# A float32 cross-attention kernel: q is loaded ahead of the first keys' lifts, and the scores of head 1 stand behind the following context product

## The reference

```python
query = hidden_states @ Wq
keyt = enc @ Wk
valt = enc @ Wv
hs = _mha(query, keyt, valt)            # softmax(q k^T / sqrt(80)) v, per head
ca_q1 = jnp.einsum('btc,th->bch', ca, Wq_ca)[:, indices, :]
ca_hs1 = _mha(ca_q1, residual, residual)
ca_hs2 = _mha(ca_hs1 @ Wq, ca @ Wk_ca, ca @ Wv_ca)
out = (hs + ca_hs2) @ Wout + b_out + residual
```

## Time and profile before

| | us |
|---|---|
| median of 3 runs | 1008.68 |
| lowest and highest | 1005.97, 1013.66 |
| the profiled execution, its own time | 1004.1 |
| its span, from the first to the last instruction | 1002.4 |

### The profile page before, as it was taken

How to read it: one execution, slowest core, us unless ns; L and a number is a source line. 1 busy time by engine, 2 the same in 40 slices (tenths; PEclk the granted TensorE clock), 3 DMA queues, 4 the chain that set the end, 5 groups by cost and what they waited for, 6 DMA issues and landing times.

```text
span 1002.4 us, 20729 instructions
## 1 busy us (share of the span) xinstructions
PE 983.8 (98%) x6740; PEld 964.2 (96%) x6740; DVE 645.5 (64%) x1129; ACT 490.0 (49%) x895; POOL 343.5 (34%) x286
## 2 busy tenths in 40 slices
PE   9999799999999999999999999999999999999998
PEld 9998699999999999999999999999999999998997
DVE  6444556676667766767676767676766666667444
ACT  7433445555454546464646463646454545546110
POOL 5212254424251616151524243343343343416000
PEclk9899999999999999999999999999999999999999
DMA  7989967797978797979797978888787878795354
GB/s 266 258 285 279 259 131 203 168 196 172 195 172 191 174 182 178 185 184 179 185 186 176 186 191 169 202 174 201 161 208 157 206 163 202 168 216 156 97 181 146
DMA packets 154169, 190.12 MB, mean 190 GB/s; under 512 B 80928, under 2 KB 108192, under 8 KB 154144
## 3 DMA queue, kind: packets, MB, share of 16 engines
q1 hardware_dynamic: 147456, 177.44, 75.9%
q10 hardware_dynamic: 6688, 12.35, 3.7%
HBM read 81.56 MB, written 19.95 MB: 101 GB/s over the span
## 4 chain that ended last, share of the span: by engine, by line
PE 85%; SPq 5%; DMA 4%; DVE 3%; ACT 2%; issue 1%; ACTq 0%
PE psS L750 22%; PE psB L785 20%; PE psB L790 10%; PE psS L725 8%; PE psT L766 6%; PE psS L894 6%; PE psT L812 4%; PE psT L818 2%; SPq L382 2%; DMA kstack<-kT 1%; PE psB L867 1%; PE psB L844 1%; SPq L379 1%; PE psT L819 1%; PE psS L950 1%
## 5 line engine op out<-in xcount | busy, mean ns | idle before, releaser
L750 PE MATMUL psS<-encT_keep,Wk_keep 128*128 128x360 f32 x1440 | 255.3, 330 | 2.8 <-ACT probs L1133 2.8
L750 PEld LDWEIGHTS psS<-encT_keep,Wk_keep 128*128 128x128 f32 x1440 | 238.7, 189 | 3.9 <-issue 3.3
L785 PE MATMUL psB<-PT_h,encN_h 120*128 120x400 f32 x576 | 202.3, 351 | 0.0
L785 PE MATMUL psB<-PT_l,encN_h 120*128 120x400 f32 x576 | 198.8, 345 | 0.0
L1133 ACT ACTIVATE probs<-psS,negmax 100x718 f32<-100x718 f32 x128 | 110.2, 861 | 131.8 <-DVE negmax L1524 131.6
L612 POOL TENSOR_TENSOR encT_keep<-encT_raw,encT_keep 128x718 fp32r<-128x718 f32 x45 | 79.7, 1770 | 184.6 <-ACT encT_keep L1162 182.2
L1548 DVE TENSOR_TENSOR kT<-psS,kT 128x718 fp32r<-128x718 f32 x80 | 72.4, 905 | 105.7 <-ACT kT L1157 105.7
L620 POOL TENSOR_TENSOR encN_l<-enc_raw,encN_h 120x768 fp32r<-120x768 f32 x48 | 92.4, 1926 | 93.5 <-ACT encN_h L1169 92.1
L603 POOL TENSOR_TENSOR Mbd<-Mbd,fmask 128x320 fp32r<-128x320 f32 x48 | 47.0, 978 | 221.4 <-DMA Mbd<-m_split 218.8
L1157 ACT ACTIVATE kT<-psS 128x718 fp32r<-128x718 f32 x80 | 61.7, 771 | 123.4 <-PE psS L750 109.9
L790 PE MATMUL psB<-PT_h,encN_l 120*128 120x400 f32 x576 | 120.4, 344 | 0.7 <-POOL encN_l L620 0.7
(11 more groups left out here) (245 smaller groups left out, 1635.8 us busy)
## 6 DMA issues: line engine op xcount, KB each, us to landing
kstack<-kT SPq DMA_DIRECT2D x64, 448.8 KB
kstack<-kT SPq DMA_DIRECT2D x192, 112.2 KB
enc_raw<-in_encN_dram SPq DMA_DIRECT2D x48, 360.0 KB, 5.5
encT_raw<-in_encT_dram SPq DMA_DIRECT2D x45, 359.0 KB, 6.0
kstack<-kT SPq DMA_DIRECT2D x32, 359.0 KB
kstack<-kT SPq DMA_DIRECT2D x32, 269.2 KB
kstack<-kT SPq DMA_DIRECT2D x32, 179.5 KB, 3.6
kstack<-kT SPq DMA_DIRECT2D x64, 89.8 KB, 3.9
```

What stands on the lines that cost most here:

```text
L750: mm = pe.matmul(keys_in(f, first)[:, half, 0:HALF], w[:, c, f * 128:(f + 1) * 128], e[:, c, k0:k0 + HALF], start=(j == 0), stop=(j == 3 * ...
L785: pe.matmul(psB[:, 1, 0:RH], eN[0][:, k, cc], PT[p][:, k, rows], start=(k == 0 and p == 0), stop=False)
```

## The change

SyncE issues `load_q(i + 1)` ahead of `lift(i + 1, 0)` in the batches that are not the first. Head 1 of the next batch leaves the end of `batch(i)` on PE, ACT and DVE and goes into the start of `batch(i + 1)`: `scores(i, 1)` behind `context(i - 1, 2)`, `expo(i, 1)` behind `u_high(i - 1, 2)`, `rowmax(i, 1)` behind `u_low(i - 1, 2)`. On DVE `norm(i, 1)` also goes behind `k_low(i, 3)`. No instruction is added or removed, and no wait.

```diff
--- before.py
+++ after.py
@@ -528,9 +528,9 @@
                         if not last:
                             store_hs(i - 1, 1)
                     if not last:
-                        lift(i + 1, 0)
                         if not first:
                             load_q(i + 1)
+                        lift(i + 1, 0)
                         lift(i + 1, 1)
                         if first:
                             sp.wait_ge(s["q"], NP * GROUPS)
@@ -1005,6 +1005,7 @@
                 def batch(i, first=False, last=False):
                     if not first:
                         context(i - 1, 2)
+                        scores(i, 1)
                     keys(i, 3)
                     if not first:
                         values(i - 1, 0)
@@ -1069,7 +1070,6 @@
                         context(i, 1)
                         scores(i + 1, 0)
                         b2_scores(i + 1, 1)
-                        scores(i + 1, 1)
 
                 pe.wait_ge(s["warm"], 2)
                 warm = gbd[:, 0:4, :].rearrange("p h j -> p (h j)")
@@ -1296,6 +1296,7 @@
                 def batch(i, first=False, last=False):
                     if not first:
                         u_high(i - 1, 2)
+                        expo(i, 1)
                     k_high(i, 3)
                     if first:
                         store_q2(4, FT)
@@ -1396,7 +1397,6 @@
                         u_high(i, 1)
                         expo(i + 1, 0)
                         b2_exp(i + 1)
-                        expo(i + 1, 1)
 
 
                 for c in range(2):
@@ -1685,8 +1685,9 @@
                     b2_norm(i)
                     if not first:
                         u_low(i - 1, 2)
+                        rowmax(i, 1)
+                    k_low(i, 3)
                     norm(i, 1)
-                    k_low(i, 3)
                     if first:
                         q_low(3, 0)
                     else:
@@ -1761,7 +1762,6 @@
                         u_low(i, 1)
                         rowmax(i + 1, 0)
                         b2_less_max(i + 1, 1)
-                        rowmax(i + 1, 1)
 
 
                 nc.vector.memset(st2[:, 0, :], 0.0).then_inc(s["warm"], 1)
```

## The result

The changed kernel takes 1016.74 us in the median of 18 runs (1013.27 to 1022.95), the kernel before 1009.35 in 18 runs taken beside it. The ratio is 1.0075, 95% interval 1.0058 to 1.0092: slower by 0.75%, some 7.6 us. One of the 18 executions of the kernel before took 2957 us; without it their median would be 1008.68. The forecast was 1.8%, 18 us. The sign and the mechanisms were right, the size was not, and the main reason is one term of the sum.

What follows compares the result with a forecast made beforehand. PE, busy 983.8 of 1002.4 us, was taken to bound the kernel. 14 x (1.0 + 0.3) = 18.2, plus 0.3 and 0.4, less 1.0, gave +17.9, rounded to 18: 1008.7 + 18 = 1027 us, range 1012 to 1038.

Steps and rivals of the forecast that it cites:

- at most 1.0 us could be won: In the loop, 14 batches at 52.00 us against the best batch's 51.93 leave at most 1.0 us to gain.
- the waits at `values`: PE's weight load of `values` waits for `u_low(i, 2)` behind `b2_norm`; the change removes this, gaining 1.0 us.
- Part 1: At the batch boundary, q issued ahead of the lift of f = 0: about 1.0 us lost in each of 14 batches.
- 0.8 us in hand: Before L832's second half on PE: `b2_less_max(0)` is done 0.85 us early, so some 1.0 of 1.8 us remains.
- The shares of 0.76 and 1.04: DMA shares at the boundary, lift f = 0 at 0.76, then q at 1.04; read as trace agreement on queue order.
- a landing near 506.5: Estimate from the skill page alone for the lift at the boundary: lands near 506.5, without any wait.
- I take 1.8: Lateness of `k_high(i + 1, 2)` behind the lift at each loop boundary, taken from the end of batch 0: 1.8 us.
- The bounds in the text, 0 to 1.5: Cost per boundary of the later lift: 0 if it lands after 2.4 us, about 1.5 us if after 6.8.
- Part 2: Head 1's scores behind `context(i - 1, 2)` uncover the psB evacuation: 0.6 us a batch alone, 0.3 behind a stalled L832.
- the +0.4 of the last batch: In the last batch, SyncE's lifts and the load of Wout follow `hs_add`, maybe 0.4 us later: +0.4 once.
- A: At the boundaries, the lift lands in time and only lost cover costs, 0.6 a batch: +8.4, 1017 us; chance 0.20.

Runs made afterwards that it cites:

- e3: The kernel before, with only `u_low(i - 1, 2)` moved ahead of `b2_norm(i)` on DVE: 1007.96 us, ratio 0.9991.
- e4: The kernel before, with the six small DMAs of `load_ga(i + 1)` moved ahead of `lift(i + 1, 0)` on SyncE: 1033.34 us, ratio 1.0253.
- e6: The kernel before, with q of the next batch issued by ACT behind `expo(i, 7)` instead of by SyncE: 1017.21 us, ratio 1.0109.
- e2: The changed kernel with the lift ahead of q as before, so only head 1's scores moved: 1013.15 us, ratio 1.0055.
- e1: The kernel before, with only `load_q(i + 1)` ahead of `lift(i + 1, 0)`, head 1's scores at their old place: 1013.86 us, ratio 1.0057.

## Why the prediction was wrong in size and right in kind

- **What bounds the kernel, and that at most 1.0 us could be won**: right for the execution that it was read from. In e3 the waits at `values` are gone, and its loop is 0.6 us shorter over 13 periods than in that execution.
- **Part 1, the mechanism**: right in each link: the lift behind q's bytes, `k_high(2)` waiting for the DMA, 0.8 us in hand, then L832. The conversion held: 1.16 late gives 0.38 at L832 (1.16 - 0.79 = 0.37). e4 shows that at least 0.7 us of the 1.16 are due to q's transfers and not to the later issue. The rule of the Trainium skill that the forecast weighed ("DMA: Bandwidth & Descriptors", section "Queues, rings and completion order"), that a DMA engine takes the descriptors of one ring in order, agrees with the changed kernel, where only q's packets move up to 508.8, and with e4 beside it; e6 adds that being in another queue doesn't free the lift of it. The shares of 0.76 and 1.04 that the forecast names as agreement tell how busy the transfer engines were, not in which order they worked. The fixed cost of about 2.0 us, from the same page of the Trainium skill, stands in a section ("Anatomy of one DMA") on DMAs that GpSimd issues, while the lifts are issued by SyncE; a landing near 506.5, without any wait, did not come, as the lift was late in every batch.
- **Part 1, the size: this is the step that failed.** "I take 1.8": I took the lateness from one row, the end of batch 0 in one execution. The loop measured 1.16 (0.8 to 2.0 in single batches). It is the landing that was too long: from the start of the lift's last issue to that of `k_high(2)` the forecast has 6.26 + 0.11 = 6.37 us, and the loop measured 5.24 in the mean (4.6 to 6.4), while that issue came 0.5 us later against the transposes than forecast. After the 0.79 in hand, 1.8 leaves 1.0 and 1.16 leaves 0.38, so an error of a half in the lateness became a factor of two and a half in the cost. The bounds in the text, 0 to 1.5, did hold the measured value; but the landings of the earlier trace rows, from which they come, are of other lifts (the page's list of issues has landings only for pieces of 179.5, 89.8 and 44.9 KB, and none of f = 0), so that this is in part luck. The middle was wrong, and I gave the chance to a single sample because its surroundings were alike.
- **Part 2**: right. 0.5 to 0.7 for itself, 0.52 measured in e2 at every boundary. Behind part 1 I had left it 0.3; it is 0.71 - 0.38 = 0.33. What the forecast put at nothing is what PE loses after a wait: 0.18 us at L832 when part 1 is alone (e1), 0.1 at the second product of `context(2)`.
- **What was taken at zero**: `expo(1)` ahead of `k_high(3)`, `norm(1)` behind `k_low(3)` show no wait on PE; the +0.4 of the last batch did not come: from `keys(15, 3)` to the end are 121.2 us before and after.
- **The sum**: 14 x (0.38 + 0.33) = 9.9 with the measured lateness, which is what the repeated profiles show for the loop. It leaves out two things that nearly cancel, the 0.1 a batch of the second product (+1.4) and the waits at `values` (-1.0). The medians differ by 7.4 (interval of the ratio: 5.9 to 9.3 us). What takes off the other 2 us I can't show; the stretch ahead of the loop varies by more than that from profile to profile, and the kernel before had medians of 1007.61 and 1007.48 us in the 35 and 17 executions beside the experiments, against 1009.35 here; against those the changed kernel is some 9 us slower.
- **The rivals**: A's time, 1017 us, is what came, but not A's way. A said that the lift lands in time; it is late in every batch. A's 0.6 a batch and the true 0.71 are near each other because the two losses lie partly under each other: that A's time is right is luck.

## What to carry to other kernels

When two waits end at the same engine, price them as one chain with what is in hand, not as a sum; and when a price is "lateness minus slack", put the spread of the lateness through it before choosing a middle, as one sample near the slack says little. A move on the engine with the highest load is free only if the moved work wasn't the cover of something: look for whose evacuation ran beside it. Before putting a load early in a queue, ask how much it sets ahead of the next one, and what in that queue has least in hand.

## What the runs showed that I had not expected

The landing of one and the same group of DMAs at the same place of the program varied so that the engine behind it was 0.7 to 2.1 us late over twelve profiles, and 0.70, 1.73 and 1.84 us late in the three of the kernel before. Six small DMAs (100 KB) ahead in SyncE's list cost 25 us over the kernel, more than q's 750 KB did, as they pushed q, which had little in hand, and head 1's lift behind it. And after a wait of PE, the second product starts 0.28 us behind the first where 0.18 is usual; in e1 the third is late as well, so a short stall cost 0.1 to 0.2 us more than its length.
